# Who splits the attention outputs of a pair's last round: VectorE instead of POOL

## The chip, the core and the metric

The kernel runs on one core of one Trainium2 chip. Its time is the device time of one execution in microseconds, the median of three runs. A core has five engines with queues of their own: TensorE (PE, matmuls, with weight loads shown as PEld), VectorE (DVE), ScalarE (ACT), GpSimd (POOL) and SyncE (SP), which only issues DMAs. They order themselves by semaphores.

## The reference

One decoder layer for 32 sequences of 100 tokens and 256 features: self-attention, cross-attention and a routed feed-forward, each on a layer-normalised input and added to it. The change lies in self-attention:

```python
def _L0_attn_ref(x, wq, wk, wv, wo):          # 16 heads of 64
    xq = jnp.einsum('bsh,oh->bso', x, wq)     # likewise xk, xv
    xq = xq.reshape(bsz, N_HEADS, seqlen, HEAD_DIM)
    scores = jnp.einsum('bhid,bhjd->bhij', xq, xk) * SCALE
    scores = jax.nn.softmax(scores, axis=-1)
    out = jnp.einsum('bhij,bhjd->bhid', scores, xv)
    out = out.reshape(bsz, seqlen, N_HEADS * HEAD_DIM)
    return jnp.einsum('bso,ho->bsh', out, wo)
x = x + _L0_attn_ref(_layernorm(x), L0_attn_wq, L0_attn_wk, L0_attn_wv, L0_attn_wo)
```

Note that the reshapes cut the token-major rows into heads without a transpose, so that a head is made of the projections of some six tokens.

## The kernel before

Self-attention, cross-attention and the experts run one after the other. To keep float32 precision, the weight products are done as three matmuls with numbers that are split into leading and trailing bits (`hi`, type fp32r, and `lo = src - hi`); `split3`, lines 62 to 66, is the helper that issues the three, so lines 64, 65 and 66 stand for every such product.

Self-attention works on quads of 4 sequences, 8 quads in all. A quad first makes its queries, keys and values (fills, line 64 with `ps_p`; `heads_out` and `spread`, line 308, bring them from PSUM to `q_t` and `k_t`, half by ScalarE, half by VectorE). Then come 8 rounds in software pipeline. A round holds two groups of 4 heads, one of each sequence of a pair; rounds 0 to 3 are the first pair of sequences, rounds 4 to 7 the second. In iteration r of the loop (it runs to 10):

- TensorE makes the scores of round r (line 745), the products with the values of round r-2 (line 763), the transposed scores of round r-1 (line 785) and their shift by the row maximum (line 789, with `diag`), and the transposes of the normalised outputs of round r-2 into `ps_ot` (line 799).
- VectorE takes the row maximum of round r (line 634), then reciprocal and `o_norm` of round r-2 (lines 642, 646), and at the end of the iteration prepares keys of round r+2 (`pair_keys`, line 275).
- ScalarE takes the exponential of round r-1 (line 453), copies the turned outputs of round r-2 out of `ps_ot` into `stage` with four copies (line 463), and prepares keys and queries of round r+2.
- POOL splits the outputs of round r-3 (`split_outputs`, lines 528 and 530: a cast to `o_hi`, a subtraction to `o_lo`), then makes `diag` of round r (line 542).

When a pair's last round (3 or 7) has been split, in iterations 6 and 10, TensorE ends the iteration with the pair's projection: 2 sequences by 8 tiles by 3 matmuls, into `ps_p` for the first pair and `ps_ot` for the second. VectorE then adds it to `x_all` (line 659). In iterations 8 to 10 TensorE also makes the first four fills of the next quad, except in the last quad; in iteration 10 three of these fills stand ahead of the projection, and on VectorE their spread copies stand ahead of what iteration 10 has besides. Fills wait until both engines have drained the bank.

`stage` holds the turned outputs of two rounds, so that ScalarE's copies of a round wait for the split of the round two before. In `stage` the 8 feature tiles t of one token lie side by side; the split writes `o_hi` and `o_lo` by tile with the tokens side by side, 25 in a round, so that it reads with a step of 8 floats. POOL's and VectorE's queues are in program order; the order of the work is written out by hand as above.

Of the kernel before, what the change touches and what calls it, by code (L numbers as in the profile page):

```python
# [7 lines left out]
F32 = mybir.dt.float32  # L8
# [3 lines left out]
ALU = mybir.AluOpType  # L12
# [14 lines left out]
GB = H1 // GH  # L27
GQ = QUAD * GB
ROWS = S * O1 // HD1
NT = O1 // 128  # L30
# [124 lines left out]
def self_attention(nc, c, x, wqkT, wvT, woT, v_dram, xs, cross):  # L155
# [5 lines left out]
    with ExitStack() as ctx:  # L161
# [6 lines left out]
        def sem(name):  # L168
            return ctx.enter_context(nc.semaphore(name))
# [26 lines left out]
        o_hi = sb("o_hi", [128, 2, NT, S], F32R)  # L196
        o_lo = sb("o_lo", [128, 2, NT, S], F32R)
        SQ = S // GB
        o_part = c.stage[:, 2 * KD * O1 - 4 * SQ * NT:2 * KD * O1].rearrange("p (u g c) -> p u g c", u=2, g=2)
# [10 lines left out]
        dve_passed = c.dve_passed  # L210
# [34 lines left out]
        ot_copied_act = sem("ot_copied_act")  # L245
        o_hi_ready = sem("o_hi_ready")
        o_lo_ready = sem("o_lo_ready")
        y_ready = sem("y_ready")
        x1_ready = sem("x1_ready")

# [33 lines left out]
        ROUNDS = GQ // 2  # L284
# [10 lines left out]
        def in_round(r):  # L295

            return (2 * r, 2 * r + 1) if 0 <= r < ROUNDS else ()

        def last_round_of_pair(r):
            return 0 <= r < ROUNDS and r % GB == GB - 1  # L300

        def spread(copy, f, a):

# [94 lines left out]
        @block.scalar  # L398
        def _(act):

            def high_bits(n):
                act.wait_ge(piece_loaded[n], 16)
                act.copy(columns(w_hi, *PIECES[n]), columns(w_stage, *PIECES[n])).then_inc(w_hi_ready, 1)

            def leading_bits(q):
                for k in range(KD):
                    act.wait_ge(filled, q * FILLS + (k + 1))
                    act.copy(x_hi[:, k], bank(k)[:, 0:QT_TOK]).then_inc(drained_act, 1)

            def heads_out(q, f):  # L410
                act.wait_ge(filled, q * FILLS + (PLACE[f] + 1))
                spread(act.copy, f, 0).then_inc(drained_act, 1)

            def values_out(q, f):
                i, v = value_slot(f)
                act.wait_ge(filled, q * FILLS + (PLACE[f] + 1))
                if i >= 2:
                    act.wait_ge(v_stored[i - 2], q * 16 + 16)
                else:
                    reach(act, v_stored[i + 2], q * 16)  # L420
                act.copy(v_tok[0:64, i % 2, 512 * v:512 * (v + 1)], bank(f)[0:64, :]).then_inc(drained_act, 1)

            def round_operands(q, r):
                if r >= 2:
                    act.wait_ge(scores_ready, q * GQ + 2 * (r - 1))
                pair_keys(act.copy, r, 0).then_inc(k_pair_act, 1)
                act.copy(q_hi[:, r % 2], q_t[:, r // GB, GH * S * (r % GB):GH * S * (r % GB + 1)]
                         ).then_inc(q_hi_ready, 1)

            def quad(q, last):  # L430
                for f in body_fills():
                    if f < FV:
                        heads_out(q, f)
                    else:
                        values_out(q, f)
                act.wait_ge(drained_act, q * FILLS + ROUNDS_FROM)
                act.wait_ge(drained_dve, q * FILLS + ROUNDS_FROM)
                if isinstance(q, int) and q == 0:
                    act.wait_ge(pairs_cleared, 1)
                round_operands(q, 0)  # L440
                for r in range(-1, ROUNDS + TAIL):
                    for f in values_in(r):
                        values_out(q, f)
                    if r == ROUNDS and not last:
                        leading_bits(q + 1)
                    for f in AHEAD.get(r, ()):
                        if not last:
                            heads_out(q + 1, f)
                    for g in in_round(r - 1):
                        act.wait_ge(shifted_ready, q * GQ + (g + 1))  # L450
                        if g >= 2:
                            act.wait_ge(pv_ready, q * GQ + (g - 1))
                        act.activation(probs[:, g % 2], ps_t[g % 2][0:S, 0:GH * S], ACT.Exp,  # L453
                                       scale=HD1 ** -0.5).then_inc(probs_ready, 1)
                    for g in in_round(r - 2)[0:1]:
                        act.wait_ge(ot_ready, q * GQ + (g + 2))
                        if isinstance(q, int) and q == 0 and r - 2 < 2:
                            act.wait_ge(vo_lo_ready, 4)
                        else:
                            act.wait_ge(o_lo_ready, q * ROUNDS + (r - 3))  # L460
                        for a in range(2):
                            for odd in range(2):
                                act.copy(*turned_part(r - 2, a, odd)).then_inc(ot_copied_act, 1)  # L463
                    if -1 <= r < ROUNDS - 2:
                        round_operands(q, r + 2)

            high_bits(0)
            high_bits(1)
            leading_bits(0)
            high_bits(2)  # L470
            high_bits(3)
            for f in range(FQ, FQ + 4):
                heads_out(0, f)
            quad(0, False)
            with act.Fori(1, QUADS - 1) as q:
                quad(q, False)
            quad(QUADS - 1, True)

        @block.gpsimd
        def _(pool):  # L480
# [38 lines left out]
            def split_outputs(q, r):  # L519

                s0 = SQ * (r % GB)
                hi, lo = (t[:, :, :, s0:s0 + SQ] for t in (o_hi, o_lo))
                src = o_part[:, r % 2].rearrange("p g (s t) -> p g t s", t=NT)
                pool.wait_ge(ot_copied_act, q * 2 * GQ + 4 * (r + 1))
                if r % GB == 0:
                    reach(pool, y_ready, q * QUAD + 2 * (r // GB))
                pool.sem_inc(pool_passed, 1)
                pool.tensor_copy(hi, src).then_inc(o_hi_ready, 1)  # L528
                pool.wait_ge(o_hi_ready, q * ROUNDS + (r + 1))
                pool.tensor_tensor(lo, src, hi.bitcast(F32), ALU.subtract).then_inc(o_lo_ready, 1)  # L530

            def quad(q, last):
                if not last:
                    inverse_root(q + 1)
                for r in range(ROUNDS + TAIL):
                    if r >= 3:
                        split_outputs(q, r - 3)
                    for g in in_round(r):
                        pool.wait_ge(max_ready, q * GQ + (g - g % 2 + 2))
                        if g >= 2:  # L540
                            pool.wait_ge(shifted_ready, q * GQ + (g - 1))
                        pool.tensor_tensor(diag[:, g % 2],  # L542
                                           c.neg_ident[0:S, 0:S].unsqueeze(1).to_broadcast([S, GH, S]),
                                           row_max[:, g // 2 % 2, g % 2].unsqueeze(2).to_broadcast([S, GH, S]),
                                           ALU.mult).then_inc(diag_ready, 1)
# [8 lines left out]
        def _(dve):  # L554
# [35 lines left out]
            def heads_out(q, f):  # L590
                dve.wait_ge(filled, q * FILLS + (PLACE[f] + 1))
                spread(dve.tensor_copy, f, 1).then_inc(drained_dve, 1)

            def values_out(q, f):
# [4 lines left out]
                else:  # L599
                    reach(dve, v_stored[i + 2], q * 16)  # L600
                dve.tensor_copy(v_tok[64:S, i % 2, 512 * v:512 * (v + 1)],
                                bank(f)[64:S, :]).then_inc(drained_dve, 1)

            def quad(q, last):
                for f in body_fills():
                    if f >= FV:
# [21 lines left out]
                for r in range(-1, ROUNDS + TAIL):  # L628
# [22 lines left out]
                    for f in AHEAD.get(r, ()):  # L651
                        if not last:
                            heads_out(q + 1, f)
                    for g in in_round(r - 3):
                        if last_round_of_pair(r - 3):
                            i = batch_of(g)
                            dve.wait_ge(y_ready, q * QUAD + (i - i % 2 + 2))
                            xb = at_batch(c.x, q * QUAD + i, slice(0, D))
                            dve.tensor_tensor(xb, ps_y[i // 2][0:S, D * (i % 2):D * (i % 2 + 1)], xb,
                                              ALU.add).then_inc(x1_ready, 1)  # L660
# [15 lines left out]
        def _(pe):  # L676
# [30 lines left out]
            def quad(q, last):  # L707
# [24 lines left out]
                for r in range(-1, ROUNDS + TAIL):  # L732
# [69 lines left out]
                    for g in in_round(r - 3):  # L802
                        if last_round_of_pair(r - 3):
                            i = batch_of(g)
                            pe.wait_ge(o_lo_ready, q * ROUNDS + (r - 2))
                            if i >= 2:
                                pe.wait_ge(x1_ready, q * QUAD + 2)
                            if isinstance(q, int) and q == 0:
# [1590 lines left out]
```

## Time and profile before

| what | us |
|---|---|
| median of 3 runs | 1483.98 (1481.58 to 1489.32) |
| the profiled execution, its own time | 1482.46 |
| its span in the profile | 1480.7 |
| TensorE busy | 1377.8 (93%) |
| VectorE busy | 947.8 (64%) |
| ScalarE busy | 759.1 (51%) |
| POOL busy | 651.1 (44%) |

Busy times are sums over the whole span; self-attention takes the first 645 us of it, 8 quads of about 77 us. Granted TensorE clock over the span: 0.976 of full speed. How an instruction's row is read: its start in us from the span's start, its length, engine, line, operation, output and input with shapes, how often it stands there in a row, and in brackets how long the engine was idle before it and who released it.

### The profile page before, as it was taken

Reading aid. Unit: us, or ns where it says so; the run is one execution under the profiler, and the core shown is the slowest. Engines: PE = TensorE matmul, PEld = TensorE weight load, DVE = VectorE, ACT = ScalarE, POOL = GpSimd, SP = SyncE. Lnnn points to the kernel's source line nnn. Section 1 sums busy time; section 2 is a strip of 40 time slices with the busy share of each in tenths; the row PEclk is TensorE's granted clock in tenths of the full one; section 3 lists DMA queues with packets and bytes.
Section 4 is the critical chain, followed back from the end, with each engine's and each line's share of the span. In section 5 each row is a group of like instructions: output and inputs, shape, how many; then the busy total and the mean of one; then the engine's idle time right before and its main releaser. Section 6 shows DMA issues by size and latency. Waiting matters only on the chain. (4 is left out here: it accounts for less than half of the span.)

```text
span 1480.7 us, 39048 instructions
## 1 busy us (share of the span) xinstructions
PE 1377.8 (93%) x12162; PEld 1193.0 (81%) x12162; DVE 947.8 (64%) x2409; ACT 759.1 (51%) x1882; POOL 651.1 (44%) x1001
## 2 busy tenths in 40 slices
PE   6999999999999999958999999999999976999997
PEld 4888878787879787847888888888888865888887
DVE  6757474748575756536777777777777755655554
ACT  4747464646555556523565655656556541222222
POOL 4634344352616161732335555555555542333332
PEclk9999999999999999978999999999999987999999
DMA  6606152433425252527766767667766653666662
GB/s 194 156 1 164 35 134 61 112 83 78 117 59 136 55 140 47 152 77 206 197 185 176 193 191 197 186 176 195 190 194 186 163 189 99 220 215 215 208 222 70
DMA packets 181117, 217.44 MB, mean 147 GB/s; under 512 B 83487, under 2 KB 148934, under 8 KB 180775
## 3 DMA queue, kind: packets, MB, share of 16 engines
q1 hardware_dynamic: 176424, 209.60, 51.0%
q0 software_dynamic: 3584, 6.58, 1.4%
q8 instruction: 44, 0.72, 0.2%
q10 hardware_dynamic: 1024, 0.21, 0.1%
q14 instruction: 41, 0.33, 0.1%
HBM read 137.62 MB, written 79.43 MB: 147 GB/s over the span
## 5 line engine op out<-in xcount | busy, mean ns | idle before, releaser
L1476 DVE TENSOR_REDUCE row_max<-psb_s 100x1 f32<-100x361 f32 x512 | 265.4, 531 | 142.5 <-PE psb_s L1692 136.7
L1346 ACT ACTIVATE probs<-psb_t 121x400 f32<-121x400 f32 (+1 forms) x384 | 190.3, 507 | 88.0 <-PE psb_t L1702 81.8
L1692 PE MATMUL psb_s<-k,q 97*100 97x362 f32 x512 | 185.5, 364 | 14.0 <-DVE row_max L1476 7.9
L542 POOL TENSOR_TENSOR diag<-neg_ident,row_max 100x400 fp32r<-100x400 f32 x128 | 112.9, 904 | 169.5 <-DVE row_max L634 140.6
L1702 PE MATMUL psb_t<-q,k 98*121 98x200 f32 (+1 forms) x768 | 146.3, 273 | 1.8 <-ACT probs L1346 1.7
L1702 PEld LDWEIGHTS psb_t<-q,k 98*121 98x121 f32 (+1 forms) x768 | 125.4, 184 | 4.8 <-ACT probs L1346 2.4
L453 ACT ACTIVATE probs<-ps_t 100x400 f32<-100x400 f32 x128 | 57.5, 501 | 114.9 <-PE ps_t L789 114.9
L1692 PEld LDWEIGHTS psb_s<-k,q 97*100 97x100 f32 x512 | 85.9, 168 | 33.9 <-DVE row_max L1476 18.6
L2179 ACT ACTIVATE hid<-psd_h,b_sb 128x256 f32<-128x256 f32 (+1 forms) x100 | 43.1, 431 | 112.8 <-PE psd_h L2293 112.7
L1715 PE MATMUL psb_o<-probs,v_ext 121*32 121x100 f32 (+1 forms) x3072 | 92.7, 253 | 0.0
L528 POOL CAST o_hi<-stage 128x400 fp32r<-128x400 f32 x64 | 60.1, 940 | 72.6 <-ACT stage L463 33.4
L308 ACT COPY q_t<-ps_p 64x200 f32<-64x200 f32 x112 | 57.0, 509 | 64.2 <-PE ps_p L66 63.4
L64 PE MATMUL ps_p<-x_lo,w_hi 128*128 128x400 f32 x224 | 82.2, 367 | 4.7 <-DVE q_t L308 0.2
L634 DVE TENSOR_REDUCE row_max<-ps_s 100x4 f32<-100x400 f32 x128 | 67.6, 571 | 28.3 <-PE ps_s L745 27.8
L463 ACT COPY stage<-ps_ot 64x200 f32<-64x200 f32 x256 | 81.8, 319 | 6.1 <-PE ps_ot L799 1.2
L2293 PE MATMUL psd_h<-h_in,w_sb 128*128 128x256 f32 (+1 forms) x448 | 82.0, 340 | 2.6 <-ACT h_in L2165 1.4
L530 POOL TENSOR_TENSOR o_lo<-stage,o_hi 128x400 fp32r<-128x400 f32 x64 | 81.9, 1279 | 5.1
L1715 PEld LDWEIGHTS psb_o<-probs,v_ext 121*32 121x32 f32 (+1 forms) x3072 | 64.4, 110 | 21.4 <-issue 15.9
L2293 PEld LDWEIGHTS psd_h<-h_in,w_sb 128*128 128x128 f32 x448 | 72.4, 193 | 11.3 <-issue 1.8
L2304 PE MATMUL psd_y<-w_sb,hid 128*128 128x256 f32 x352 | 80.4, 379 | 0.0
L66 PE MATMUL ps_p<-x_hi,w_hi 128*128 128x400 f32 x224 | 77.5, 346 | 0.0
L65 PE MATMUL ps_p<-x_hi,w_lo 128*128 128x400 f32 x224 | 77.0, 344 | 0.0
(255 smaller groups left out, 3742.8 us busy)
## 6 DMA issues: line engine op xcount, KB each, us to landing
w_sb<-in_w SPq DMA_DIRECT2D x28, 1024.0 KB, 7.5
routed_rows<-empty SPq DMA_DIRECT2D x7, 3855.0 KB, 18.2
packed_keys<-k_st SPq DMA_DIRECT2D x32, 724.0 KB, 4.1
k<-packed_keys SPq DMA_DIRECT2D x64, 362.0 KB
v_rows<-v_tok SPq DMA_DIRECT2D x32, 400.0 KB
v_ext<-v_rows SPq DMA_DIRECT2D x32, 400.0 KB
q<-packed_queries SPq DMA_DIRECT2D x64, 200.0 KB
w_third<-in_w SPq DMA_DIRECT2D x12, 1024.0 KB, 7.6
```

Of the source, the lines that this page charges most:

```text
L64: pe.matmul(out, hi_l, lo_r, start=first, stop=False)
L66: return pe.matmul(out, hi_l, hi_r, start=False, stop=last)
L463: act.copy(*turned_part(r - 2, a, odd)).then_inc(ot_copied_act, 1)
L530: pool.tensor_tensor(lo, src, hi.bitcast(F32), ALU.subtract).then_inc(o_lo_ready, 1)
L542: pool.tensor_tensor(diag[:, g % 2], c.neg_ident[0:S, 0:S].unsqueeze(1).to_broadcast([S, GH, S]), row_max[:, g // 2 % 2, g % 2].unsqueeze( ...
L1346: act.activation(probs[0:KT[kt], u % 2, kt], ps_t[i % 2][0:KT[kt], 0:4 * S], ACT.Exp, scale=HD2 ** -0.5).then_inc(probs_ready, 1)
L1476: dve.reduce_max(row_max[:, p, h:h + 1], ps_s[h % 2][0:S, 0:S2], AX_X).then_inc(max_ready, 1)
L1692: pe.matmul(ps_s[h % 2][0:S, 0:S2E], q2[0:97, p, u, g, S * a:S * (a + 1)], k2[0:97, p, u, g], start=True, stop=True).then_inc(scores_ready, 1)
L1702: ins = pe.matmul(ps_t[i % 2][0:n, 2 * S * g:2 * S * (g + 1)], k2[:, p, u, g, rows], q2[:, p, u, g], start=True, stop=True)
L1715: ins = pe.matmul(ps_o[32 * h:32 * (h + 1), S * u:S * (u + 1)], v_ext[0:n, p, kt, 4 * u + h, :], probs[0:n, u % 2, kt, S * h:S * (h + 1)], ...
L2293: ins = pe.matmul(ps_h[f % 4][:, 0:UNIT * nh], w1_sb[j % 3][:, k, 128 * f:128 * (f + 1)], h_in[:, j % 2, k, 0:UNIT * nh], start=(k == 0), ...
L2304: ins = pe.matmul(ps_y[n % 3][:, 0:D], hid[:, f, UNIT * t:UNIT * (t + 1)], w2_sb[j % 3][:, f, :], start=(f == 0), stop=(f == NF - 1))
```

## The change

The split of a pair's last round, 3 and 7, is issued by VectorE (`split_last`), in iterations 6 and 10, after `o_norm` and after the spread copies of the next quad's fills, and before the wait for the projection. POOL splits the other six rounds of a quad. A semaphore `last_split` counts VectorE's two instructions; `split_by_pool` and `split_by_dve` give the counts that the waits want. TensorE's projection waits for both semaphores, ScalarE's copies for the one that belongs to the round two before.

```diff
+        last_split = sem("last_split")
...
+        def split_by_pool(q, r):
+
+            return q * BY_POOL + (r + 1 - (r + 1) // GB if r >= 0 else 0)
+
+        def split_by_dve(q, r):
+
+            return q * 2 * PAIRS + 2 * ((r + 1) // GB)
...
+                        elif r - 4 == -1 or last_round_of_pair(r - 4):
+                            act.wait_ge(last_split, split_by_dve(q, r - 4))
                         else:
-                            act.wait_ge(o_lo_ready, q * ROUNDS + (r - 3))
+                            act.wait_ge(o_lo_ready, split_by_pool(q, r - 4))
...
                 for r in range(ROUNDS + TAIL):
-                    if r >= 3:
+                    if r >= 3 and not last_round_of_pair(r - 3):
                         split_outputs(q, r - 3)
...
+            def split_last(q, r):
+
+                s0 = SQ * (r % GB)
+                hi, lo = (t[:, :, :, s0:s0 + SQ] for t in (o_hi, o_lo))
+                src = o_part[:, r % 2].rearrange("p g (s t) -> p g t s", t=NT)
+                dve.wait_ge(ot_copied_act, q * 2 * GQ + 4 * (r + 1))
+                dve.sem_inc(dve_passed, 1)
+                dve.tensor_copy(hi, src).then_inc(last_split, 1)
+                dve.wait_ge(last_split, split_by_dve(q, r) - 1)
+                dve.tensor_tensor(lo, src, hi.bitcast(F32), ALU.subtract).then_inc(last_split, 1)
...
                     for f in AHEAD.get(r, ()):
                         if not last:
                             heads_out(q + 1, f)
+                    if last_round_of_pair(r - 3):
+                        split_last(q, r - 3)
                     for g in in_round(r - 3):
...
-                            pe.wait_ge(o_lo_ready, q * ROUNDS + (r - 2))
+                            pe.wait_ge(o_lo_ready, split_by_pool(q, r - 3))
+                            pe.wait_ge(last_split, split_by_dve(q, r - 3))
```

## Rows read from the trace of the kernel before

**Rows 1.** The page's span and its line of busy times.

```profile
span 1480.7 us, 39048 instructions
...
PE 1377.8 (93%) x12162; PEld 1193.0 (81%) x12162; DVE 947.8 (64%) x2409; ACT 759.1 (51%) x1882; POOL 651.1 (44%) x1001
```

**Rows 2.** TensorE's waits, 0 to 645 us: total, times, longest.

```profile
PE ps_ot L64 <- POOL o_lo L530: 13.5, 8, 3.8
...
PE ps_p L64 <- POOL o_lo L530: 10.6, 8, 1.4
PE ps_s L745 <- DVE row_max L634: 2.6, 8, 0.4
```

**Rows 3.** Timeline of TensorE in the third quad.

```profile
210.70 0.60 PE L789 MATMUL ps_t<-diag,ones_r 100*100 100x400 f32 x2
...
225.17 0.61 PE L789 MATMUL ps_t<-diag,ones_r 100*100 100x400 f32 x2
...
227.45 0.36 PE L64 MATMUL ps_p<-w_lo,o_hi 128*100 128x256 f32 x1 [1.32 <-POOL o_lo L530]
```

**Rows 4.** Timeline of POOL and ScalarE in the third quad.

```profile
211.20 1.66 POOL L542 TENSOR_TENSOR diag<-neg_ident,row_max 100x400 fp32r<-100x400 f32 x2 [1.86 <-PE ps_t L789]
...
223.52 1.66 POOL L542 TENSOR_TENSOR diag<-neg_ident,row_max 100x400 fp32r<-100x400 f32 x2
...
226.16 1.24 POOL L530 TENSOR_TENSOR o_lo<-stage,o_hi 128x400 fp32r<-128x400 f32 x1
...
222.79 1.35 ACT L463 COPY stage<-ps_ot 64x200 f32<-64x200 f32 x4
```

**Rows 5.** Timeline of VectorE in the third quad.

```profile
224.61 0.42 DVE L646 TENSOR_TENSOR o_norm<-ps_p,recip 100x256 f32<-100x256 f32 x1
233.53 0.76 DVE L659 TENSOR_TENSOR x_all<-ps_p,x_all 100x256 f32 x2 [8.49 <-PE ps_p L66]
```

**Rows 6.** VectorE's instructions by line: ns min/median/max, first and last start.

```profile
L275 DVE CAST k_pair<-k_t x64: 357/366/1033, 46.6 to 609.4; 64x400 fp32r<-64x400 f32 x64
...
L587 DVE TENSOR_TENSOR x_lo<-ps_s,x_hi x16: 562/572/577, 14.8 to 551.5; 128x400 fp32r<-128x400 f32 x16
...
L308 DVE COPY q_t<-ps_p x112: 481/517/542, 22.2 to 586.4; 64x200 f32<-64x200 f32 x112
...
L646 DVE TENSOR_TENSOR o_norm<-ps_o,recip x64: 423/424/426, 55.3 to 629.6; 100x256 f32<-100x256 f32 x64
```

**Rows 7.** POOL's casts by line; the last row is the page's (busy us, mean ns).

```profile
L1145 POOL CAST c_hi<-c_t x16: 784/784/787, 648.1 to 1162.8; 128x722 fp32r<-128x722 f32 x16
...
L496 POOL CAST w_hi<-stage x4: 1028/1034/1040, 23.6 to 34.0; 128x1024 fp32r<-128x1024 f32 x4
...
L528 POOL CAST o_hi<-stage 128x400 fp32r<-128x400 f32 x64 | 60.1, 940 | 72.6 <-ACT stage L463 33.4
```

**Rows 8.** Timeline at 217 us, VectorE and POOL.

```profile
217.83 0.72 DVE L275 CAST k_pair<-k_t 64x400 fp32r<-64x400 f32 x1
...
217.39 0.93 POOL L528 CAST o_hi<-stage 128x400 fp32r<-128x400 f32 x1
```

**Rows 9.** Timeline at the end of the second quad: VectorE, POOL, TensorE.

```profile
170.55 1.03 DVE L308 COPY k_t<-ps_p 64x200 f32<-64x200 f32 x2
...
170.60 1.24 POOL L530 TENSOR_TENSOR o_lo<-stage,o_hi 128x400 fp32r<-128x400 f32 x1
...
171.89 0.36 PE L64 MATMUL ps_ot<-w_lo,o_hi 128*100 128x256 f32 x1 [1.38 <-POOL o_lo L530]
```

**Rows 10.** Timeline at the end of the last quad: ScalarE, TensorE.

```profile
631.23 1.35 ACT L463 COPY stage<-ps_ot 64x200 f32<-64x200 f32 x4 [1.22 <-PE ps_ot L799]
...
635.01 0.54 PE L64 MATMUL ps_ot<-w_lo,o_hi 128*100 128x256 f32 x1 [3.81 <-POOL o_lo L530]
```

**Rows 11.** Busy times by stretch; the figure before the DMA share is the granted clock.

```profile
304.59:312.19 7.60, 7.60 (x51) 7.60 (x52) 0.00 (x1) 0.28 (x1) 1.57 (x2) 0.78 0.34 73
...
635.01:639.50 4.49, 4.49 (x22) 4.49 (x23) 0.00 (x0) 0.00 (x0) 0.00 (x0) 0.52 0.00 0
```

More of the change, by code:

```diff
@@ L300, in last_round_of_pair @@
             return 0 <= r < ROUNDS and r % GB == GB - 1
+        PAIRS = ROUNDS // GB
+        BY_POOL = ROUNDS - PAIRS
+        def split_by_pool(q, r):
+            return q * BY_POOL + (r + 1 - (r + 1) // GB if r >= 0 else 0)
+        def split_by_dve(q, r):
+            return q * 2 * PAIRS + 2 * ((r + 1) // GB)
         def spread(copy, f, a):
@@ L528, in split_outputs @@
                 pool.tensor_copy(hi, src).then_inc(o_hi_ready, 1)
-                pool.wait_ge(o_hi_ready, q * ROUNDS + (r + 1))
+                pool.wait_ge(o_hi_ready, split_by_pool(q, r))
                 pool.tensor_tensor(lo, src, hi.bitcast(F32), ALU.subtract).then_inc(o_lo_ready, 1)
```

## The prediction

> **What bounds the kernel now.** The page is read first: TensorE is busy for 93% of the span, VectorE 64%, POOL 44% [rows 1]. A busy share doesn't say where this change is paid, so the next view is TensorE's waits over self-attention, the first 645 us of the span. Apart from the start, only two groups are worth anything: the first matmul of a pair's projection (line 64) waits for `o_lo`, eight times for bank `ps_p` (10.6 us, at most 1.4 each) and eight times for `ps_ot` (13.5 us, seven of about 1.38 and one of 3.8) [rows 2]. The first eight are the projections in mid quad (round 3's pair, one in each of 8 quads), the other eight those at a quad's end (round 7's pair). Nothing else of self-attention waits for more than 2.6 us in total, so what TensorE gains or loses there moves everything behind it, cross-attention and experts too. The change can touch 24.1 us of 1480.7.
>
> **The mid-quad wait.** In the third quad TensorE stands idle for 1.32 us after its last transposes; the projection begins at 227.45, at the moment when POOL's subtraction ends (226.16 + 1.24 = 227.40) [rows 3, 4]. The data was there long before: ScalarE's four copies ended at 222.79 + 1.35 = 224.14 [rows 4]. POOL was late, since the second `diag` of round 5 held it until 223.52 + 1.66, about 225.19; then it took 0.94 for the cast and 1.24 for the subtraction [rows 4, 7]. VectorE, in contrast, ends its last `o_norm` at 224.61 + 0.42 = 225.03 and then idles 8.49 us to the projection's end [rows 5]. So there the work moves to an idle engine.
>
> **What one split costs on VectorE.** No row shows it; bounds come from near ones. Cast: VectorE's float32 to fp32r cast of 400 elements, from SBUF to SBUF, takes 366 ns (median). Subtraction: 400 elements, one input from PSUM, 572 ns [rows 6]. Those read runs that lie together, while the split reads `stage` with a step of 8 floats (32 bytes). Rows on what a step costs: POOL casts 722 adjacent elements in 784 ns and 1024 in 1034 (0.83 ns each, so 400 would take about 517), but the stepped 400 of `o_hi` take 940, 1.06 ns more for each. VectorE's spread copies write 200 elements with a step of 16 floats in 517 ns, where a line through 256 in 424 and 400 in 572 gives 366: 0.75 ns more for each [rows 6, 7]. I take 0.8 ns for each element that VectorE reads by this step, nearest to its own row: subtraction 0.57 + 0.32 = 0.89; cast 0.37 + 0.16 = 0.53 (it moves two elements in the time in which the subtraction moves one, so half the addition). The ends are no addition (0.37 and 0.57) and 1.06 ns (0.57 and 0.99, or 0.79 for the cast if it pays in full). With 0.05 us from `o_lo` to TensorE (227.40 to 227.45) [rows 3, 4] and about as much, 0.04, taken ahead of each instruction of VectorE, a split runs 1.55 us; ends 1.07 and 1.9.
>
> The Trainium skill prices the same two instructions by length and number of SBUF inputs alone ("VectorE: DVE Perf Modes", "The TRN2 errata" and "The perf-mode tier table"): float32 copies at twice the rate, two-input operations at (N + 151)/0.96 ns, which is 574 ns for 400. By it the step would cost nothing; that is the first rival.
>
> **Port.** VectorE's cast `k_pair` at 217.83 took 0.72 instead of 0.37: POOL's cast ran from 217.39 to 218.32 and VectorE ended 0.23 later [rows 8]. The longest such cast took 1.03, always across a POOL instruction [rows 6]. So VectorE stands still while POOL's instruction runs, and only 0.14 of its fixed part lies beside it.
>
> **Mid quad, summed.** VectorE's cast is issued at 225.07, POOL's `diag` ends at 225.19, the cast ends 0.23 + 0.16 later at 225.58. Subtraction from 225.62 to 226.51, projection at 226.56 instead of 227.45: 0.89 gained, in 8 quads 7.1 us. POOL's next instruction is now `diag` of round 6, no longer queued behind a split. It waits for round 5's shift, which TensorE starts at 225.17; a released `diag` begins 0.50 after that (210.70, 211.20), so at 225.67, 0.05 behind VectorE's subtraction [rows 3, 4]. I let the earlier one have the port. The `diag` is then late by 0.8 us, hidden by 6 us of projection. The added wait on TensorE queues only the projection and what follows, which waited there before; ScalarE's copies two rounds later wait for a split that ended microseconds before. VectorE's `x_all` sums stand behind the split but wait for the projection anyway. No DMA or SP queue is passed. POOL's rounds 4 to 6 are as before.
>
> **Quad end, summed.** Here the order on VectorE decides. The split stands in its queue behind three spread copies for the next quad's fills. Before, POOL was free, and ended its subtraction at 170.60 + 1.24 = 171.84; TensorE started at 171.89. VectorE ends the last spread at 170.55 + 1.03 = 171.58, and only then can cast [rows 9]. 171.58 + 1.55 = 173.13: 1.24 later, in the seven quads that prefill the next one 8.7 us lost (ends 0.76 and 1.6 each, 5.3 and 11). In the last quad nothing is in front: ScalarE ends at 631.23 + 1.35 = 632.58, and TensorE started at 635.01 [rows 10]; VectorE, begun 0.12 after ScalarE, makes it 634.21, 0.8 gained (ends 0.4 and 1.3).
>
> **The granted clock.** After two of the eight mid-quad gaps the projection ran at 0.78 on average: 7.6 us (304.59 to 312.19) against 6.08 (227.45 to 233.53), 1.5 lost each [rows 3, 5, 11]; after the last gap of 3.8 us it fell to 0.52, near the lower level of 1.2 GHz, for 4.5 us, about 2 us lost (4.5 us at half speed do the work of 2.3) [rows 11]. After the seven quad-end gaps of 1.38 no projection was longer. With the mid gap down from 1.3 to 0.4 I take the two losses away, -3.0. The quad-end gaps grow to 2.6, between one that never cost anything and one that did: two or three of seven at 1.5, +4 (ends 0 and 14).
>
> Sum: -7.1 + 8.7 - 0.8 - 3.0 + 4 = +1.8 us. On the profiled execution's own 1482.46 (span 1480.7 and 1.8 around it) that is 1484.3; the median of the runs shown lies 1.5 above that execution, so 1485.8, said as **1486**.
>
> **Rival 1, the step costs VectorE nothing.** Cast to 225.42, subtraction 225.46 to 226.03: the whole listed mid gap goes, 10.6. Quad ends cost 0.76 x 7 = 5.3, the last gives 1.3: -6.6, with -3.0 of clock and +1 for gaps of 2.1: -8.6, or 1475.4. For it: no row shows a stepped read on VectorE. Against it: the rows of two engines with a step both cost more. 27%.
>
> **Rival 2, slower: POOL takes the port first in mid quad.** It decides where VectorE's subtraction asks for its port after 225.67. My margin is 0.05; a cast of 0.57 takes it, and so does a request made only when data moves. Then `diag` runs 0.83 to 226.50, the subtraction ends 0.89 - 0.14 = 0.75 later at 227.25, the projection starts at 227.30: 0.15 gained for each, 1.2 in all. -1.2 + 8.7 - 0.8 + 4 = +10.7, and the two clock losses stay: 1494.7; with the dear ends of the split up to 1499. For it: `diag` runs 0.83 once released, and the margin is thin; against it: VectorE is first by my times. 30%. The Trainium skill ("SBUF — State Buffer", "SBUF: two separate sides") says the same of this port: an exclusive lock for the whole instruction, to the one that starts first. The 0.72 us cast agrees; no row here has two that start within 0.1 us.
>
> **Chances.** My case 38% (own range 1479 to 1491), rival 1 27%, rival 2 30%, other 5%. A measurement of this kernel tells about 0.5%, 7.4 us, from no change, so faster is under 1476.6 and slower over 1491.4: faster 0.23 (most of rival 1), same 0.43, slower 0.34 (most of rival 2 and a tail of mine with more clock losses). The range of eight in ten, from rival 1's middle to rival 2's: 1474 to 1497.
>
> **What would show it.** In mid quad a `last_split` cast and subtraction of 0.5 and 0.9 us on VectorE near 225, `diag` directly behind, and TensorE's gap near 0.4; a subtraction of 1.6 is rival 2, one of 0.57 rival 1. At quad ends the gap must grow from 1.38 to about 2.6, with VectorE's spread, cast and subtraction back to back. If it doesn't grow, the reading of VectorE's queue is wrong. If the quad-end projections all stay near 6.07, my clock term is wrong and the sum falls by 4. Beyond 645 us nothing should differ.

## The result and the profile after

| | median us | runs |
|---|---|---|
| before | 1482.44 (1479.40 to 1492.68) | 20 |
| after | 1489.89 (1487.64 to 1492.74) | 20 |

The changed kernel takes 1.0048 times as long (95% interval 1.0036 to 1.0061): slower by about 7 us, inside the range and on the side on which the forecast lay, though the change that was forecast was +1.8 us. The profiled execution after took 1487.64, the shortest of its 20; that of before, 1482.46, stood at its median. So the two profiles differ by 5.0 us of span, a little less than the medians do.

The waits of TensorE over self-attention are the view that shows the change at once (total us, times, longest):

```profile
PE ps_ot L64 <- DVE o_lo L627: 15.5, 6, 2.6
...
PE ps_ot L64 <- issue: 5.7, 2, 3.1
...
PE ps_p L64 <- DVE o_lo L627: 3.1, 7, 0.5
...
PE ps_p L64 <- issue: 0.4, 1, 0.4
```

Against [rows 2]: the mid-quad wait fell from 10.6 to 3.1 + 0.4 = 3.5 us, the wait at the quad ends rose from 13.5 to 15.5 + 5.7 = 21.2. A wait for two semaphores goes by the name of the later one, and two rows carry "issue" where the profile shows no releaser; added up by bank they are the same eight and eight.

Third quad, mid quad, timelines of VectorE, POOL and TensorE (to be held against [rows 3 to 5]):

```profile
226.68 0.68 DVE L625 CAST o_hi<-stage 128x400 fp32r<-128x400 f32 x1
227.39 0.88 DVE L627 TENSOR_TENSOR o_lo<-stage,o_hi 128x400 fp32r<-128x400 f32 x1
...
225.28 1.66 POOL L556 TENSOR_TENSOR diag<-neg_ident,row_max 100x400 fp32r<-100x400 f32 x2
227.41 2.35 POOL L556 TENSOR_TENSOR diag<-neg_ident,row_max 100x400 fp32r<-100x400 f32 x2 [0.47 <-PE ps_t L816]
...
228.33 0.36 PE L64 MATMUL ps_p<-w_lo,o_hi 128*100 128x256 f32 x1 [0.48 <-DVE o_lo L627]
```

VectorE's cast waits for the end of POOL's `diag` (225.28 + 1.66 = 226.94) and then needs 0.42 more; the subtraction follows and is first at the port by 0.02 us; POOL's pair of `diag` takes 2.35 instead of 1.66 because of it, which nobody waits for. TensorE's gap is 0.48.

Second quad, quad end, VectorE and TensorE (against [rows 9]):

```profile
169.75 1.00 DVE L320 COPY k_t<-ps_p 64x200 f32<-64x200 f32 x2
170.78 0.52 DVE L625 CAST o_hi<-stage 128x400 fp32r<-128x400 f32 x1
171.33 0.88 DVE L627 TENSOR_TENSOR o_lo<-stage,o_hi 128x400 fp32r<-128x400 f32 x1
...
172.27 0.54 PE L64 MATMUL ps_ot<-w_lo,o_hi 128*100 128x256 f32 x1 [2.56 <-DVE o_lo L627]
```

The last spread copy, the cast and the subtraction stand back to back, and TensorE has waited 2.56 us instead of 1.38. What then happens to the projection is in the stretches (the figure before the DMA share is the granted clock, a mean over the stretch as a share of 2.4 GHz); the first and third are quad ends at a lowered clock, the second one that kept it:

```profile
172.27:179.68 7.41, 7.41 (x50) 7.41 (x51) 0.00 (x1) 0.00 (x0) 0.00 (x0) 0.80 0.00 0
251.10:257.17 6.07, 6.07 (x50) 6.07 (x51) 0.00 (x0) 0.00 (x0) 0.00 (x0) 1.00 0.00 0
...
328.46:336.06 7.60, 7.59 (x50) 7.60 (x51) 0.00 (x1) 0.00 (x0) 0.00 (x0) 0.78 0.00 0
```

Five of the seven quad-end projections are long here (7.3 to 7.6 us, 7.0 us over 6.07 each in sum), none in mid quad.

The difference of the two profiles by parts: mid gaps -7.1, quad-end gaps +8.5, gap of the last quad -0.75, mid clock -3.0, quad-end clock +7.0, clock of the last projection -0.4, start -0.5. That makes +3.8, and the last sum of self-attention did move from 642.90 to 646.72, by 3.8. The remaining 1.2 us lie behind it, where neither code nor counts changed (837.8 to 839.0 us). Over the ten profiles of this document that part took 837.6 to 843.6 us, and TensorE's busy time in it 782.7 to 788.6: it scatters by more than these 1.2 us, so a difference of a few us between two single executions need not come from the edit.

### The profile page after: what moved, and what is told of

Same layout as the page of the kernel before. It is cut to its first block and busy times, and to the rows that moved or that the text cites. A ratio compares the mean times of both kernels' runs of the same rounds, so it can differ in the third digit from the quotient of the medians.

```text
span 1485.7 us, 39082 instructions
## 1 busy us (share of the span) xinstructions
PE 1382.5 (93%) x12162; PEld 1197.2 (81%) x12162; DVE 969.3 (65%) x2441; ACT 760.1 (51%) x1882; POOL 622.2 (42%) x969
## 5 line engine op out<-in xcount | busy, mean ns | idle before, releaser
L556 POOL TENSOR_TENSOR diag<-neg_ident,row_max 100x400 fp32r<-100x400 f32 x128 | 117.7, 941 | 179.9 <-DVE row_max L659 147.0
L2332 PEld LDWEIGHTS psd_y<-w_sb,hid 128*128 128x128 f32 x352 | 65.4, 190 | 8.1
L542 POOL CAST o_hi<-stage 128x400 fp32r<-128x400 f32 x48 | 44.5, 927 | 61.4 <-PE ps_p L66 37.4
```

Of the source, the lines that this page charges most:

```text
L556: pool.tensor_tensor(diag[:, g % 2], c.neg_ident[0:S, 0:S].unsqueeze(1).to_broadcast([S, GH, S]), row_max[:, g // 2 % 2, g % 2].unsqueeze( ...
L2332: ins = pe.matmul(ps_y[n % 3][:, 0:D], hid[:, f, UNIT * t:UNIT * (t + 1)], w2_sb[j % 3][:, f, :], start=(f == 0), stop=(f == NF - 1))
```

## The experiments

Each time of before was measured on the same chip beside the run. Every diff is against the changed kernel, and `...` stands for what is left out of it. A ratio is measured over all runs of both kernels and can differ by 1 to 2 us from the difference of the medians. Theory: what counts is how late TensorE's projection gets its `o_lo` at the two places, and the clock that a longer gap costs. Rivals: VectorE's work or the shared port as such; another cause of the long projections.

**Mid quad alone.** VectorE splits round 3 only:

```diff
-        PAIRS = ROUNDS // GB
-        BY_POOL = ROUNDS - PAIRS
+        BY_DVE = (GB - 1,)
+        BY_POOL = ROUNDS - len(BY_DVE)
...
-                    if r >= 3 and not last_round_of_pair(r - 3):
+                    if r >= 3 and r - 3 not in BY_DVE:
...
-                    if last_round_of_pair(r - 3):
+                    if r - 3 in BY_DVE:
                         split_last(q, r - 3)
```

> VectorE splits round 3 of each quad only (the pair that ends in mid quad); POOL splits round 7 again. Theory (queue): the changed kernel's gain sits wholly in mid quad and its loss wholly at the quad ends, so this keeps the mid gap at 0.42 us and brings the quad-end gap back to 1.38 us. 8 x 0.9 = 7.2 us gained, and up to 3 us of granted clock that the mid gap of 1.3 cost: 7 to 10 us below the kernel before, near 1474. Rival (any split on VectorE costs by what it adds to VectorE's work and to the port that it shares with POOL): then half of the change's loss stays, and this is 2 to 4 us above the kernel before.

Measured 1475.24 against 1481.8, ratio 0.9964 (0.9947 to 0.9981): 6.6 us by the medians and 5.3 by the ratio, short of the 7 to 10. TensorE's waits:

```profile
PE ps_ot L64 <- POOL o_lo L544: 13.6, 8, 3.8
...
PE ps_p L64 <- DVE o_lo L627: 3.1, 7, 0.5
```

Gaps of 0.42 to 0.49 in mid quad, 1.37 to 1.42 at the quad ends as before; no projection but the last long. This half of the change is a gain; the rival, which had the time rise, is out. The gaps alone make 7.1 us, so nothing of the 3 us of clock that the prediction added in mid quad shows in the medians.

**Quad end alone**, the same edit with `BY_DVE = (ROUNDS - 1,)`:

> VectorE splits round 7 only; POOL splits round 3 as before. Queue theory: mid gap 1.32 again, quad-end gap 2.6: 7 x 1.2 = 8.7 us lost, about 7 us more through the lower granted clock after five of the seven gaps (the profile of the changed kernel), 0.8 gained in the last quad: 13 to 16 us above the kernel before, near 1497. Rival as for e1: about 4 us above.

Measured 1491.07 against 1481.8, ratio 1.0069 (1.0056 to 1.0082): slower by 9 to 10 us, less than 13 to 16. The gaps are as expected (2.58 to 2.63), 7.7 us with the last quad's; so about 1.5 is left for the clock by the median, where 7 had been expected. In the profile, which fell on the longest of its five runs (1496.71), three of the seven projections were long and cost 5.5 us together, half of it in one:

```profile
487.45:496.26 8.81, 8.81 (x50) 8.81 (x51) 0.00 (x0) 0.00 (x0) 0.00 (x0) 0.65 0.00 0
```

The gap term held. The clock term had been taken over from the changed kernel's profile, and with the mid gap at 1.3 again it came out smaller; the section on why the prediction was right comes back to this.

**The order in VectorE's queue.** The changed kernel with the quad-end split ahead of the last two fills' spread copies (two instructions each):

```diff
-                    for f in AHEAD.get(r, ()):
-                        if not last:
-                            heads_out(q + 1, f)
+                    ahead = [] if last else list(AHEAD.get(r, ()))
+                    late = ahead[1:] if last_round_of_pair(r - 3) else []
+                    for f in ahead[:len(ahead) - len(late)]:
+                        heads_out(q + 1, f)
                     if last_round_of_pair(r - 3):
                         split_last(q, r - 3)
+                    for f in late:
+                        heads_out(q + 1, f)
```

> The changed kernel, but at the quad end VectorE splits after the first of the three spread copies, not after the third. Queue theory: the split starts at about the end of ScalarE's copies (169.4 in the second quad of the kernel before) and ends 1.5 later at 170.9, against POOL's 171.84: quad-end gap near 0.4 us, 7 x 0.96 = 6.7 gained there, 7.2 in mid quad, 0.8 in the last quad, 3 of clock: 15 to 18 us below the kernel before, near 1466. Rival (the delayed spreads come due): the two late spread copies hold up TensorE's next fills behind the projection by 1 to 1.5 us, the gap only moves, and the time is that of e1 or up to 3 us above it.

Measured 1465.95 against 1481.8, ratio 0.9906 (0.9892 to 0.9921): 15.9 us by the medians, 13.9 by the ratio, for the expected 15 to 18. VectorE at the second quad's end:

```profile
165.20 1.03 DVE L320 COPY k_t<-ps_t 64x200 f32<-64x200 f32 x2 [0.38 <-PE ps_t L66]
166.34 0.58 DVE L625 CAST o_hi<-stage 128x400 fp32r<-128x400 f32 x1
166.96 0.90 DVE L627 TENSOR_TENSOR o_lo<-stage,o_hi 128x400 fp32r<-128x400 f32 x1
167.77 1.02 DVE L320 COPY q_t<-ps_p 64x200 f32<-64x200 f32 x2
```

The same two instructions, four copies (two fills) earlier: the quad-end gap is 0.55 to 0.63, all seven projections take 6.1 us or less, and the delayed copies delay nobody. The loss of the change was its place in VectorE's queue.

**The price of the step.** The split reads `stage` side by side; the features of rounds 3 and 7 come out in another order, so this kernel computes something else in the same number of instructions of the same sizes:

```diff
-                src = o_part[:, r % 2].rearrange("p g (s t) -> p g t s", t=NT)
+                src = o_part[:, r % 2].rearrange("p g (t s) -> p g t s", t=NT)
```

> The changed kernel with VectorE's split reading stage side by side instead of with a step of 8 floats, so that the features of rounds 3 and 7 come out in another order; sizes and instructions are the same. Theory (a step costs VectorE about 0.8 ns an element): cast 0.52 becomes 0.37 us, subtraction 0.88 becomes 0.57; the quad-end gap 2.6 becomes 2.1 and the mid gap 0.42 becomes nearly 0: 7 x 0.5 + 8 x 0.4 = 6.7 us below the changed kernel, more if fewer projections run at the lower clock (up to 7): 1476 to 1483. Rival (the two lengths have another reason, such as the 128 partitions or the port): they stay at 0.52 and 0.88, and so does the time, 1490.

VectorE's two lines in the changed kernel, then in this one (ns min/median/max):

```profile
L625 DVE CAST o_hi<-stage x16: 518/521/679, 70.6 to 637.7; 128x400 fp32r<-128x400 f32 x16
L627 DVE TENSOR_TENSOR o_lo<-stage,o_hi x16: 873/882/891, 71.1 to 638.3; 128x400 fp32r<-128x400 f32 x16
```

```profile
L625 DVE CAST o_hi<-stage x16: 368/401/505, 70.2 to 629.4; 128x400 fp32r<-128x400 f32 x16
L627 DVE TENSOR_TENSOR o_lo<-stage,o_hi x16: 575/576/577, 70.6 to 629.8; 128x400 fp32r<-128x400 f32 x16
```

The step costs 306 ns for the 400 elements of the subtraction (0.77 each) and 150 for the cast's shortest. The kernel took 1480.62 against before's 1481.8, ratio 0.9996 (0.9984 to 1.0009): so the world of rival 1, where the step costs nothing, would have been no change at all. The gaps shrank as it said (quad end 2.11 to 2.15, mid quad gone), but four of seven projections were long all the same, 6.0 us in sum, where it had allowed 1 us.

**The gap filled.** In seven quad ends ten matmuls that nobody reads:

```diff
+                            if g == GQ - 2 and not last:
+                                pe.wait_ge(ot_copied_act, q * 2 * GQ + 2 * GQ)
+                                for n in range(10):
+                                    pe.matmul(ps_ot[0:S, :], x_hi[:, n % 2, 0:S], w_hi[:, 2, n % 2, 0:512],
+                                              start=True, stop=True)
```

> The changed kernel with ten matmuls of 512 columns whose results nobody reads, in seven of the quad ends, between the last fill of the next quad and the projection, after ScalarE's copies have left ps_ot: about 2.2 us of work in a gap of 2.6. Theory (after such a gap the projection runs at the lower granted clock, by the gap alone): the first matmul of the projection starts as late as before (within 0.3 us), all seven projections take about 6.07 us instead of 7.3 to 7.7 for five of them, and the time is 5 to 8 us below the changed kernel, near 1483. Rival (the long projections have another cause: weight loads, ports, what VectorE does meanwhile): some of the seven stay at 7.3 or more and the time stays at 1490 or above.

```profile
168.80 2.47 PE L835 MATMUL ps_ot<-w_hi,x_hi 128*100 128x512 f32 x10
171.63 0.36 PE L64 MATMUL ps_ot<-w_lo,o_hi 128*100 128x256 f32 x1 [0.37 <-DVE o_lo L627]
...
171.63:177.71 6.08, 6.08 (x50) 6.08 (x51) 0.01 (x1) 0.00 (x0) 0.00 (x0) 1.00 0.00 0
```

All seven projections now take 6.1 us at a granted clock of 1.00, and the time is 1481.73 against 1481.49, ratio 0.9995 (0.9983 to 1.0007). By the ratios to the kernel before that is some 8 us under the changed kernel, though TensorE does 17 us more work and starts no quad-end projection earlier: counted from the end of the mid-quad projection it starts after 16.92 us in the second quad, against 16.80 in the changed kernel. That is the clock's part of the loss, by itself.

**The port's margin.** One small reciprocal of VectorE ahead of the mid-quad split, then four (shown):

```diff
+        spare = sb("spare", [S, 4, GH])
...
                 dve.sem_inc(dve_passed, 1)
+                if r == GB - 1:
+                    for n in range(4):
+                        dve.reciprocal(spare[:, n], c.ones_f[0:S, 0:GH])
                 dve.tensor_copy(hi, src).then_inc(last_split, 1)
```

> The changed kernel with one small reciprocal of 4 elements (about 0.17 us) on VectorE ahead of the mid-quad split only. Theory (port goes to the one that asks first, and VectorE's subtraction was first by 0.05 to 0.1 us): now POOL's diag of round 6 is first, the subtraction runs 1.5 to 1.7 us instead of 0.88, the mid gap grows from 0.42 to about 1.3, and the time by 7 to 10 us, to 1498. Rival (VectorE has the port whenever it wants it): the gap grows by the 0.17 us alone, 1.4 us in all, 1491.

Measured 1491.54 against 1481.49, ratio 1.0062 (1.0045 to 1.0079), and mid gaps of 0.42 to 0.52, as if nothing had been added. The run missed its aim: the reciprocal fits into the time in which the cast would have waited for POOL's `diag`, so the subtraction still asked first (228.34 against 228.42). The time is the rival's figure, but the gap is neither theory's, so it tells them apart no better than before. Hence four:

> As e7, with four small reciprocals ahead of the mid-quad split. In e7 the one reciprocal cost nothing: VectorE's cast would have stood behind POOL's diag of round 5 meanwhile, so its subtraction still asked 0.08 us ahead of POOL's next diag (228.34 against 228.42). Three more, about 0.1 us each, put it behind. Theory (the port goes to the one that asks first): the subtraction waits out the first diag and takes 1.4 to 1.6 us instead of 0.88, and the mid gap becomes 1.1 to 1.3 us instead of 0.42; with the quad ends as they are 6 to 7 us above the changed kernel, 1496. Rival (VectorE is served first whenever it asks): the subtraction stays at 0.88, the gap is 0.7, and the time 2 to 3 us above the changed kernel.

```profile
227.44 0.54 DVE L629 CAST o_hi<-stage 128x400 fp32r<-128x400 f32 x1
228.02 1.38 DVE L631 TENSOR_TENSOR o_lo<-stage,o_hi 128x400 fp32r<-128x400 f32 x1
...
227.89 2.18 POOL L557 TENSOR_TENSOR diag<-neg_ident,row_max 100x400 fp32r<-100x400 f32 x2 [0.49 <-PE ps_t L820]
```

Now POOL's `diag` is first by 0.13 us, the subtraction takes 1.38 instead of 0.88, and the mid gap is 1.12 to 1.27. Here too the port went to the one that asked first; rival 2 was a real case, missed in the changed kernel by 0.02 us. The trace decides this, not the time: 1491.73 against 1482.96, ratio 1.0062 (1.0037 to 1.0086), is 2 us over the changed kernel by the ratios, the rival's figure, and doesn't show the 5.7 us that the mid gaps grew by. In the profile only two of its seven quad-end projections were long, against five in the changed kernel's.

**A version that is better than both.** As the third experiment, and the split goes sequence by sequence, with the first sequence's matmuls waiting for its half only:

```diff
-            return q * 2 * PAIRS + 2 * ((r + 1) // GB)
+            return q * 4 * PAIRS + 4 * ((r + 1) // GB)
...
-                dve.tensor_copy(hi, src).then_inc(last_split, 1)
-                dve.wait_ge(last_split, split_by_dve(q, r) - 1)
-                dve.tensor_tensor(lo, src, hi.bitcast(F32), ALU.subtract).then_inc(last_split, 1)
+                for g in range(2):
+                    dve.tensor_copy(hi[:, g], src[:, g]).then_inc(last_split, 1)
+                    dve.wait_ge(last_split, split_by_dve(q, r) - 3 + 2 * g)
+                    dve.tensor_tensor(lo[:, g], src[:, g], hi[:, g].bitcast(F32), ALU.subtract
+                                      ).then_inc(last_split, 1)
...
-                            pe.wait_ge(last_split, split_by_dve(q, r - 3))
+                            pe.wait_ge(last_split, split_by_dve(q, r - 3) - 2 + 2 * (i % 2))
```

> As e3 (the split ahead of the last two spread copies), and VectorE splits the two sequences of the pair one after the other, in four instructions of 200 elements; the projection of the first sequence waits for its own half only. Theory: the first half takes about 0.34 + 0.04 + 0.52 = 0.9 us against 1.47 for the whole, so the mid gap 0.45 and the quad-end gap 0.57 of e3 nearly vanish: 8 x 0.4 + 7 x 0.5 + 0.5 = 7 us below e3's 1466, near 1459; the second half is done long before the first sequence's 3 us of matmuls are. Rival (POOL's diag takes the port between the four instructions, or four fixed parts eat it up): no gain or up to 3 us slower than e3.

Measured 1458.76 against 1481.49, ratio 0.984 (0.9816 to 0.9863), as expected. Fifteen of the sixteen gaps are gone from TensorE's waits; the last quad's, with nothing to do ahead of it, is 2.5. VectorE and POOL in mid quad show the port changing hands:

```profile
219.15 0.43 DVE L626 CAST o_hi<-stage 128x200 fp32r<-128x200 f32 x1
219.61 0.54 DVE L628 TENSOR_TENSOR o_lo<-stage,o_hi 128x200 fp32r<-128x200 f32 x1
220.08 0.95 DVE L626 CAST o_hi<-stage 128x200 fp32r<-128x200 f32 x1
221.06 1.00 DVE L628 TENSOR_TENSOR o_lo<-stage,o_hi 128x200 fp32r<-128x200 f32 x1
...
219.88 1.87 POOL L556 TENSOR_TENSOR diag<-neg_ident,row_max 100x400 fp32r<-100x400 f32 x2 [0.50 <-PE ps_t L821]
```

The second half loses the port to `diag` twice (0.95 and 1.00 us instead of 0.43 and 0.54), as the rival feared, and it costs nothing: it ends at 222.06, and the first sequence's matmuls, begun at 220.21, last 3 us.

## Why the prediction was right, and where it was off

- **Mid quad, -7.1.** Expected a cast behind `diag` that ends 0.39 after it, a subtraction of 0.89, a gap near 0.4; found 0.42, 0.88 and gaps of 0.37 to 0.50, in sum -7.1. The mid-only run shows it alone.
- **Quad end, +8.5.** Expected 1.24 more for each of seven, found 1.18 to 1.26, +8.5 in sum; the reordered run shows that the place behind the spread copies is the cause. The last quad gave 0.75 for the 0.8 expected.
- **Cost of a split.** 0.53 and 0.89 were expected from bounds, 0.52 and 0.88 measured; the side-by-side run shows that the step is what lies between them and 0.37 and 0.58. The formula quoted from the Trainium skill ("VectorE: DVE Perf Modes") gives the side-by-side subtraction to 2 ns (574 to 576) and is 308 ns short with the step. The sections named there have no term for a step; that "by it the step would cost nothing" holds of them and not of the Trainium skill as a whole, so rival 1 had less behind it than its 27% say.
- **Port.** Its rule, to the first that asks, held in the changed kernel, with halves, and with four small instructions ahead. The margin was 0.02 us where 0.05 was expected, too thin to have been forecast: that mid quad came out as summed, and not as rival 2, was in part luck, as the 30% for rival 2 said. The Trainium skill's sentence ("SBUF — State Buffer", "SBUF: two separate sides") agrees: 0.88 when first, 1.38 when second by 0.13.
- **Clock, the term that was mis-sized.** The mid part held in the two profiles (-3.0, no long projection in mid quad), but the mid-only run's medians show none of it. The quad ends were put at +4, two or three of seven; this profile has +7.0, five of seven. The step that failed is the reading that a gap between one "that never cost anything and one that did" would cost in between a third of the cases, and for rival 1 that a gap of 2.1 would cost 1 us: four of seven did, 6.0 us in sum. In the four profiles with quad-end gaps of 2.6, 16 of 28 projections were long, and the term came to 2.6 to 8.6 us.
- **What the clock term left out.** It goes by the length of the quad-end gap alone. The four kernels with that gap at 2.6 differ in the mid gap, and they fall into two groups:

| | mid gap us | long of 7 | granted clock, median of all runs | time above what the gaps explain, us |
|---|---|---|---|---|
| changed kernel | 0.4 | 5 | 0.970 (20 runs) | 6.5 to 7 |
| one small instruction ahead | 0.4 | 6 | 0.969 (11) | 8.5 to 9.5 |
| quad end alone | 1.3 | 3 | 0.975 (5) | 2 to 3 |
| four small ahead | 1.1 to 1.3 | 2 | 0.973 (7) | 3 |

The kernel before stood at 0.975 to 0.977 beside the experiments. The last column is the difference to it, by ratio and by medians, less the change of all sixteen gaps. So with a short mid gap the same quad-end gap went with more long projections and a lower clock. This is a pattern over four kernels, two of them with few runs, and none was built to test it; why a shorter gap half a quad earlier should matter stays open. It fits with the halves alone, -5.3 and +10.2 by the ratios (-6.6 and +9.3 by the medians), making less than the +7 of the whole change, though that difference is within the intervals.

- **The sum.** From 1484.3 to 1487.64 on the profiled executions it is the clock term (3.0 us) and 1.2 us behind self-attention, less 0.9 of smaller terms. The change was forecast at +1.8 us and measured at some +7 over the runs; the gaps came out as summed, so most of what is missing is this clock. That the level of 1486 lies only 4 us under 1489.89 owes something to chance: its start, the median of three runs, was 1.5 us above that of twenty.

## What to carry to other kernels

Moving work to another engine pays where that engine's own queue is free at that moment, whatever its busy share says: VectorE was the busier of the two over the span (64% against 44%), and the same two instructions gained 0.9 us at one place and lost 1.2 at another, and four copies earlier in the queue they gained 0.8 there too. Read for each place what stands ahead of the new instruction in program order. Where a consumer takes its input in parts, split the producer by those parts and wait for each: it was worth a further 7 to 10 us (by the medians, and by the ratios 0.9906 and 0.984).
